# Ternary-weight sums on ScalarE instead of VectorE, and newly drawn instruction orders, in a macaron transformer kernel

## The reference

```
def _quantize(w):
    gamma = jnp.mean(jnp.abs(w))
    return jnp.clip(jnp.round(w / (gamma + EPS)), -1.0, 1.0)
...
x = x + 0.5 * _L0_ffn_ref(_layernorm(x), ...)      # silu(gate) * up, down
x = x + _L0_attn_ref(_layernorm(x), ...)           # 16 heads, rotary, causal
x = x + 0.5 * _L0_ffn_ref(_layernorm(x), ...)
x = x + 0.5 * _L1_ffn_ref(_layernorm(x), w1, w2, w3)   # sigmoid(x1) * x2, ternary
x = x + _L1_attn_ref(_layernorm(x), ...)           # 16 heads on 4 KV heads, alibi
x = x + 0.5 * _L1_ffn_ref(_layernorm(x), w1, w2, w3)
```

## Time and profile before

| | |
|---|---|
| median of 3 runs | 553.93 us (552.02 to 555.36) |
| the profiled execution's own time | 552.14 us |
| its span, first to last instruction | 550.4 us |
| PE busy | 530.6 us (96%) |
| DVE busy | 456.1 us (83%) |
| ACT busy | 401.3 us (73%) |
| POOL busy | 340.8 us (62%) |

### The profile page before, as it was taken

One profiled execution on the slowest core, in us unless ns is written; L12 is line 12 of the kernel. 1 busy time (PEld: TensorE's weight loads), 2 busy tenths in 40 slices (PEclk: granted clock), 3 DMA queues, 4 the chain that ended last, 5 costly groups with the idle time before them and its releaser, 6 DMA issues.

```text
span 550.4 us, 12977 instructions
## 1 busy us (share of the span) xinstructions
PE 530.6 (96%) x5060; PEld 302.9 (55%) x5060; DVE 456.1 (83%) x816; ACT 401.3 (73%) x603; POOL 340.8 (62%) x427
## 2 busy tenths in 40 slices
PE   8999798999999999999899999999999999999997
PEld 6676444445554654566446564465455654654664
DVE  5999999998989797699987969879997779783363
ACT  5978594878777698775886848788769676969443
POOL 2549896975987797673664364552855626545634
PEclk9999999999999999999999999999999999999999
DMA  8900110302130100410110120010211011101211
GB/s 324 355 1 2 58 58 2 116 23 62 41 103 18 43 1 2 157 42 20 63 43 2 42 83 22 22 43 6 75 36 43 1 42 64 52 2 62 80 58 38
DMA packets 22573, 31.76 MB, mean 58 GB/s; under 512 B 9408, under 2 KB 10816, under 8 KB 22360
## 3 DMA queue, kind: packets, MB, share of 16 engines
q1 hardware_dynamic: 22512, 30.94, 16.4%
HBM read 13.75 MB, written 2.36 MB: 29 GB/s over the span
## 4 chain that ended last, share of the span: by engine, by line
PE 71%; DVE 17%; ACT 4%; issue 3%; POOL 2%; SPq 1%; DMA 0%; DVEq 0%; POOLq 0%; ACTq 0%
PE PS L597 22%; PE PS L621 12%; PE PS L708 10%; PE PS L688 5%; PE PS L673 5%; DVE MX L1064 5%; PE PS L639 4%; PE PS L723 4%; PE PS L580 3%; PE PS L544 2%; PE PS L559 2%; ACT PB L850 2%; PE PS L655 2%; DVE MX L1060 1%; DVE ST L875 1%
## 5 line engine op out<-in xcount | busy, mean ns | idle before, releaser
L850 ACT ACTIVATE PB<-PS 128x1024 f32<-128x1024 f32 x160 | 158.7, 1025 | 52.9 <-PE PS L688 48.4
L1064 DVE TENSOR_REDUCE MX<-PS 128x2 f16<-128x1024 f32 (+2 forms) x192 | 158.3, 865 | 13.8 <-PE PS L544 13.1
L597 PE MATMUL PS<-XT,WGU 128*128 128x512 f16 x660 | 156.9, 380 | 4.6 <-DVE QF L1042 3.0
L1140 POOL TENSOR_TENSOR HH<-TH,HH 128x512 f16<-128x512 f32 x71 | 82.5, 1173 | 69.0 <-ACT HH L818 69.0
L1168 POOL TENSOR_SCALAR_AFFINE_SELECT PB<-PB 128x512 f32<-128x512 f32 (+1 forms) x140 | 73.8, 552 | 48.1 <-ACT PB L850 47.9
L597 PEld LDWEIGHTS PS<-XT,WGU 128*128 128x128 f16 x660 | 59.6, 98 | 75.9 <-issue 7.8
L621 PE MATMUL PS<-WD,HH 128*128 128x256 f16 x660 | 78.2, 273 | 0.4 <-POOL HH L1140 0.2
L708 PE MATMUL PS<-PB,V 128*32 128x512 f32 (+3 forms) x1024 | 75.3, 435 | 0.8 <-ACT PB L850 0.3
L621 PEld LDWEIGHTS PS<-WD,HH 128*128 128x128 f16 x660 | 62.6, 98 | 13.3 <-issue 3.3
L818 ACT ACTIVATE HH<-TH 128x512 f16<-128x512 f32 (+1 forms) x86 | 52.9, 628 | 20.2 <-PE PS L621 6.9
L673 PE MATMUL PS<-SK,SQ 63*128 63x256 f16 (+3 forms) x512 | 59.5, 299 | 5.3 <-DVE MX L1064 2.6
(11 more groups left out here) (119 smaller groups left out, 777.7 us busy)
## 6 DMA issues: line engine op xcount, KB each, us to landing
SQ<-QPB SPq DMA_DIRECT2D x24, 256.0 KB, 2.5
OC<-OT SPq DMA_DIRECT2D x16, 256.0 KB, 2.4
RB<-scratch SPq DMA_DIRECT2D x64, 64.0 KB, 2.3
SK<-QPB SPq DMA_DIRECT2D x12, 256.0 KB, 2.4
SQ<-MT SPq DMA_DIRECT2D x128, 1.0 KB
out<-X SPq DMA_DIRECT2D x8, 256.0 KB, 2.1
PB<-gu SPq DMA_DIRECT2D x2, 704.0 KB, 6.1
LATE<-gu SPq DMA_DIRECT2D x2, 704.0 KB, 14.5
```

The lines of the kernel that those rows point to most:

```text
L597: m = e.matmul(o[:, :], WGU[l][:, k, col:col + P], rows_of(f)[j][:, k, :], start=j == 0 and k == 0, stop=j == 1 and k == 1)
L850: e.activation(PB[Q % 2][:, j, :, :], two_banks("s", i), ACT.Exp, scale=0.25).then_inc(a_exp, 1)
L1064: e.tensor_reduce(mx[:, :, pr, t], o[:, :, col:col + (t + 1) * P], AX.X, ALU.max, negate=True).then_inc(a_max, 1)
L1140: e.tensor_tensor(hh[1][:, s * T:(s + 1) * T], value_of(j)[0], hh[0][:, s * T:(s + 1) * T], ALU.subtract).then_inc(f_lo, 1)
```

## The change

The sums of |w| leave VectorE. ScalarE gets a new step `B`, seven times: an activation Abs over a piece of the weights (1024, 256, 256 and four times 704 elements per partition), which writes its values to a place that nobody reads and leaves their sum in one column of `GA` by `accum_out`. A new semaphore `p_abs` counts them, and each waits for the one before. VectorE keeps the short final sums, over 4 and 2 x 2 columns instead of 22 and 2 x 22, so its string has six fewer `w`, and the values of `p_dve` are renumbered. ScalarE's `T`, which loads the table with silu, moves to the front of its string. All strings of `ORDER` and the banks are new: they come out of a search that judges an order under two sets of durations instead of one. The strings differ in places all the way to the end, but hold the same letters otherwise.

```diff
     "pe":
-        "zzzzzzzttzgGgggGGgGtzztgzGzagGgddddggGztzzgzGtGuugGaqqvgddgdvdqgGgqgtGGGguuGtqqqzmmmgmmgqmmdmmGsdsms"
...
+        "zzzzzzzttzzgggGggGzztGtGgGgGazggddddgtgGGtGGzzuuggagqzggqddzgvdGdqqvGGzgGuuGtqqtqmmmmgmqmgmdmmdsGsms"
...
     "act":
-        "wXxxTwttthtXhhthxxhtwwhtthwXthwtxwthYyyxthkhhkkvwQttQXtktvkhtYQyytQhhhxxkkkhhtwTQteQeeeeteewQQhoeete"
...
+        "TwXxxwtttwtXhthhxxBBBththhtXhBwthBwtxtwBBYxyythhhttkhttXQvtQhkkkYtQyyQxvhhhxhkQhktTwwwwQtkeeeeekehtQ"
...
-                w.wait_ge(p_dve, (8, 20)[i])
+                w.wait_ge(p_dve, (5, 13)[i])
...
+                elif c == "B":
+                    if i < 3:
+                        w.wait_ge(l_w3, 32)
+                        src = (rd[0].rearrange("p c n -> p (c n)"), rd[1][:, 0, :], rd[1][:, 1, :])[i]
+                        junk, total = TD[:, 0:(1024, 256, 256)[i]], GA[:, 2, i:i + 1]
+                    else:
+                        k, u = divmod(i - 3, 2)
+                        w.wait_ge(l_w1, 32)
+                        src, junk, total = rgu[k][:, u * HID:(u + 1) * HID], TB[1], GA[:, u, k:k + 1]
+                    w.wait_ge(p_abs, i)
+                    e.activation(junk, src, ACT.Abs, accum_out=total).then_inc(p_abs, 1)
...
-                    elif i <= 2:
-
-                        w.wait_ge(l_w3, 32)
-                        if i == 1:
-                            ga, src = GA[:, 2, 0:16], rd[0]
-                        else:
-                            ga, src = GA[:, 2, 16:20], rd[1][:, 0:1, :]
-                        e.tensor_reduce(ga, src.rearrange("p c (a b) -> p (c a) b", b=64), AX.X, ALU.add,
-                                        apply_absolute_value=True).then_inc(p_dve, 1)
-                    elif i == 3:
-
-                        e.tensor_reduce(GA[:, 2, 20:21], rd[1][:, 1:2, :], AX.XY, ALU.add,
-                                        apply_absolute_value=True).then_inc(p_dve, 1)
-                        w.wait_ge(p_dve, 5)
-                        e.tensor_scalar(GA[:, 2, 21:22], GA[:, 2, 20:21], -0.5, None, ALU.mult).then_inc(p_dve, 1)
-                        w.wait_ge(p_dve, 6)
-                        e.tensor_reduce(GS[:, 2:3], GA[:, 2, :], AX.X, ALU.add).then_inc(p_dve, 1)
-                    elif i in (4, 12):
-
-                        k = 0 if i == 4 else 1
+                    elif i == 1:
+                        w.wait_ge(p_abs, 3)
+                        e.tensor_scalar(GA[:, 2, 3:4], GA[:, 2, 2:3], -0.5, None, ALU.mult).then_inc(p_dve, 1)
+                        w.wait_ge(p_dve, 3)
+                        e.tensor_reduce(GS[:, 2:3], GA[:, 2, 0:4], AX.X, ALU.add).then_inc(p_dve, 1)
+                    elif i in (2, 6):
+
+                        k = 0 if i == 2 else 1
                         c0, c1 = ((2, 3), (0, 2))[k]
                         w.wait_ge(p_pe, k + 1)
                         e.tensor_scalar(GS[:, c0:c1], bank("a", k)[:, c0:c1], 1.0 / (HID * D), 1e-8,
                                         ALU.mult, ALU.add).then_inc(p_dve, 1)
-                        w.wait_ge(p_dve, 8 + 12 * k)
+                        w.wait_ge(p_dve, 5 + 8 * k)
                         e.tensor_scalar(GS[:, 3 + c0:3 + c1], GS[:, c0:c1], -0.5, None, ALU.mult).then_inc(p_dve, 1)
-                        w.wait_ge(p_dve, 9 + 12 * k)
+                        w.wait_ge(p_dve, 6 + 8 * k)
                         e.tensor_scalar(GS[:, c0:c1], GS[:, c0:c1], 0.5, None, ALU.mult).then_inc(p_dve, 1)
-                    elif i <= 6:
-                        k = i - 5
+                    elif i <= 4:
+                        k = i - 3
                         c0, c1 = ((0, 4), (4, 6))[k]
                         src, td = rd[k].rearrange("p c n -> p (c n)"), TD[:, 0:(c1 - c0) * D]
-                        w.wait_ge(p_dve, 10 + 2 * k)
+                        w.wait_ge(p_dve, 7 + 2 * k)
                         e.tensor_scalar(td, src, GS[:, 5:6], None, ALU.is_lt).then_inc(p_dve, 1)
-                        w.wait_ge(p_dve, 11 + 2 * k)
+                        w.wait_ge(p_dve, 8 + 2 * k)
                         e.scalar_tensor_tensor(WD[1][:, c0:c1, :].rearrange("p c n -> p (c n)"), src, GS[:, 2:3],
                                                td, ALU.is_gt, ALU.subtract).then_inc(p_dve, 1)
-                    elif i <= 10:
-                        k, u = divmod(i - 7, 2)
-                        w.wait_ge(l_w1, 32)
-                        e.tensor_reduce(GA[:, u, 11 * k:11 * k + 11],
-                                        rgu[k][:, u * HID:(u + 1) * HID].rearrange("p (a b) -> p a b", b=64),
-                                        AX.X, ALU.add, apply_absolute_value=True).then_inc(p_dve, 1)
-                    elif i == 11:
-                        w.wait_ge(p_dve, 18)
-                        e.tensor_reduce(GS[:, 0:2], GA[:, 0:2, :], AX.X, ALU.add).then_inc(p_dve, 1)
-                    else:
-                        k = i - 13
-                        w.wait_ge(p_dve, 22 + 4 * k)
+                    elif i == 5:
+                        w.wait_ge(p_abs, 7)
+                        e.tensor_reduce(GS[:, 0:2], GA[:, 0:2, 0:2], AX.X, ALU.add).then_inc(p_dve, 1)
+                    else:
+                        k = i - 7
+                        w.wait_ge(p_dve, 15 + 4 * k)
```

More of the change, by code:

```diff
@@ new lines @@
+        "msdsmdmsmgsmmpmssgmsGsmGsspsmGsmgmmpsmsmssgmmsGmmpsmsvmsvsmsmuummpqqoosmsoosssqdmsmdqtsspmmtdgggdGsG"
+        "smmgsmpmsGmsmgssgGGpmsmvmsdsmsdmsmvduudqssmqspmoottomsoggmsgGGgssmGqgmspsmqtmsgtGGpsssggddssddgmmpGG"
+        "gmmmvgvGmmuguGGoooosmqmmsqsmqmsdmsddmdsmsmsmsmspmmsmttsspsmggGgGsmgGggGGsmpmsdttsmddssmdggsmpmsmgGvg"
+        "GuGugsqmmqgGqssooGssmpmmmddddsmsosomsmmpmttsssgGgsgGmsspmsmgsmgGsmmGGgmmspsmsvdmsmddsmsdssmpmsttoosm"
+        "mgoguoguGGsmqsmqgqssmgGgGGsmmpmssdmsdmsmdsmdmpsmssmpsmttvmsggGgGGggGsmgGtsmtddmssddmsmpoosmspsouuogs"
@@ new lines @@
+        "mqmsqgGqgGssspsmmgmsvmGmmpmmggGsmsmsGsmsttmpmssddsmmdgdoooogsmsgGsmgmmmpssGssGggssspsstGGtpggGddddgg"
+        "GGgGgGooooddddttggGggGGgGGgdddd",
+    "dve":
+        "NXgtwtNhhhNktthhwhwhwhdwdknthhNwhtuuhwpqwpqdwdhpnqphqhkhhuuhtpqpqtmmmpmsmhxmmmsmdqmhxmqpmmmdmxmsmkmh"
+        "smhnmxmmsmhmcmxmsmmmhmcmxmmmuumxpqpqomoNpmmdqpqtmtcmxsshshdhmkmmsmhmmxnshshmmmcmxdmmuudNppqmqmottmox"
+        "hmkhhNmpmqhmmxcqphhttssdhdnmmshhcmkmmshmsxmshuhuoommlmmmlxmdlmdmmxNmmmmmttNmhxhkchmhhmhmxttmdmdnssmh"
+        "mmhcksshuushlmmxhsllomhmmdxmdmNommmmttxNhhmhkmmmcxhmhmmhmmxcmmdmdmnmttommxshsoushuhkmmlsllmsxhshhmmm"
+        "mdmmxmdmNmmNmxttcmhhhkhhmchtmtdmxdnmmomuumhlmxohlclkNhmmmmmhxmmmhmmxchmmttmdmmhdkxooNmhmmmmxhhchtthh"
+        "cdhhdkhhhooNdXtthkhhhdhhdd",
@@ new lines @@
+        "6035062403641053753020574757250425261046250362542063510632635730623453062540635603410641367531750432"
+        "1530153730253035152406204625351370514265021563107451250532316434062406304631576240725063214507530626"
+        "0437053204062165426054306715306143610561357015302507405270525032504275310732403516340275306235742507"
+        "4207421357135124062560432064371634760325235012460531706421254063170327341536026043602436053601346024"
+        "60247604025753024062406236406135160315072046024512062413514027561024502530126320360",
@@ L249, in macaron_kernel @@
         l_ali = [sem(f"l_ali{z}") for z in range(2)]
-        p_act, p_pool, p_dve, p_pe, p_set, p_tab, p_sc, p_gu = (sem(f"p_{n}") for n in ("act", "pool", "dve", "pe", "set", "tab", "sc", "gu"))
+        p_act, p_pool, p_dve, p_pe, p_set, p_tab, p_sc, p_gu, p_abs = (sem(f"p_{n}") for n in ("act", "pool", "dve", "pe", "set", "tab", "sc", "gu", "abs"))
         f_ln, f_ve, f_mean, f_rt, f_off, f_xn, f_xd = (sem(f"f_{n}") for n in ("ln", "ve", "mean", "rt", "off", "xn", "xd"))
@@ L564, in tensor_program @@
                     w.wait_ge(p_pool, 3)
-                    w.wait_ge(p_dve, (7, 19)[i])
+                    w.wait_ge(p_dve, (4, 12)[i])
                     c0, c1 = ((2, 3), (0, 2))[i]
@@ L589, in tensor_program @@
                     else:
-                        w.wait_ge(p_dve, 30)
+                        w.wait_ge(p_dve, 23)
                     wait_bank(w, c, i)
```

48 lines of the change are left out of this document (15 added, 33 removed).

## The result

The changed kernel takes 555.51 us (median of 16 executions, 554.46 to 556.42), the kernel before, measured beside it, 553.17 (551.83 to 555.63): ratio 1.0037 [1.0024, 1.0051]. Forecast was 551.0, and a gain. The profiled execution has a span of 553.5 us, 3.1 more than before.

What follows compares the result with a forecast made beforehand. VectorE sets the pace up to 107.8 us, TensorE behind it. Of 5.46 us removed, waits of 0.35, 1.2 and 1.0 leave 2.9: 552.14 becomes 549.2, or 551.0 us on the median's level; range 547.3 to 554.8.

Steps and rivals of the forecast that it cites:

- So of 5.46 us, 5.46 - 0.35 - 1.2 - 1.0 = 2.9 us come through to the first row maximum: VectorE's first stage: 5.46 us of sums removed, less losses at three places, brings the first row maximum 2.9 us sooner.
- POOL and SP have the same steps, and the SP queue the same DMAs ahead of each result; these cost nothing: GpSimd's steps and the DMA queue: unchanged, so no cost if the first attention's row vectors go out as early.
- I take that to stay as it is: Two VectorE threshold scalings at 0.98 us instead of 0.15: assumed unchanged, up to 1.7 us either way.
- the three I walked: Places in the first 45 us where VectorE loses time: 0.35, 1.2 and 1.0 us.
- place 2: VectorE's third gated product waits 1.2 us for TensorE's second G, now its seventh step.
- no row says which, and I take zero: Behind 107.8 us, with new strings: TensorE's 6.8 us idle time may shrink or grow; change taken as zero.
- Place 3: Third unit's transposed rows: VectorE waits about 1.0 us for ScalarE to copy them, at about 37 us.
- The upper bound of 6.6 us: ScalarE's seven sums: most they could add, with a 0.20 us activation for each read-out.
- no row of ScalarE from SBUF is slower than 1.1 ns an element: Argument against slow sums on ScalarE: profile rows show at most 1.1 ns per element from SBUF.
- TensorE's own string is packed up to the first projection: TensorE up to 46.08 us: only 0.30 us of waits, so the projection comes at most 0.3 to 0.4 us sooner.
- The third rival: Slow sums on ScalarE delay the first attention's normalized rows and chain behind; 557.3 us; chance 0.14, shared with later strings.
- The later strings lose: New orders behind 107.8 us add 3.4 us, half the idle 6.8, cancelling the gain; shares the 0.14 chance of slower.

Runs made afterwards that it cites:

- e12: Changed kernel with its first three filler steps written as 4 matmuls of 512 columns instead of 8 of 256, the same work; 553.68 us, ratio 1.0008.
- e18: Changed kernel with 5 instead of 7 fillers ahead of the first transposes; 552.97 us, ratio 1.0001.
- e6: Kernel before with VectorE's sums of |w| reading only a sixteenth of their elements, all else the same; 551.75 us, ratio 0.9979.
- e7: Changed kernel with ScalarE's seven sums cut to 64 elements each, all else the same; 554.94 us, ratio 1.0034.
- e20: Kernel before with only the sums of w1 and w2 moved into ScalarE's gaps and its table load first; 551.71 us, ratio 0.9970.
- e1: Code of the change, all seven sums on ScalarE and table load first, in the strings and banks of the kernel before; 554.40 us, ratio 1.0027.
- e14: Code of the change with the changed kernel's strings up to about 79 us, then those of the kernel before; 557.49 us, ratio 1.0071.
- e15: Code of the change with the strings of the kernel before up to about 79 us, then the changed kernel's; 557.46 us, ratio 1.0075.
- e3: Changed kernel's strings and banks with the sums back on VectorE, ScalarE's table load still first; 561.88 us, ratio 1.0163.

## Why the prediction was wrong

**The step that failed** is "So of 5.46 us, 5.46 - 0.35 - 1.2 - 1.0 = 2.9 us come through to the first row maximum". Measured is 1.58 us more distance. Two things stand in its place, and a third term, taken at zero, adds to them.

*A collision.* "POOL and SP have the same steps, and the SP queue the same DMAs ahead of each result; these cost nothing": the DMAs are the same, but one met a load of instructions, whose place no string shows. That is 1.55 us of distance and 1.6 us of time, by e12; e18 agrees.

*Nothing comes through without it either.* e12's window against that of before above:

```profile
11.05:79.97 68.92, 66.17 (x426) 41.32 (x425) 64.55 (x128) 54.69 (x97) 50.64 (x51) 1.00 0.28 109
```

The distance is the same, 68.92 and 68.89. VectorE is busy for 64.55 instead of 67.51 us: of 5.46 us removed, 2.5 came back in its other steps, and the remaining 2.96 went into idle time, 4.37 instead of 1.38. The first half is the term "I take that to stay as it is", with its bound of 1.7 us: it held two small scalings, and what grew were above all the weight comparisons, by 2.7 us together. The second half is more waits than the three I walked. The 1.49 us for TensorE (place 2) were forecast; 0.4 us each for GpSimd's x, and for ScalarE's rows, and part of a wait for the first transposed rows were not. e6 shows the second half without a new string: with only VectorE relieved, three quarters of the relief turn into its idle time.

*The strings behind.* "no row says which, and I take zero": the profiles have 473.0 us from the first row maximum to the end where before has 471.8, so 1.2 us of the 3.1 us of the longer span lie there. e12, without the collision and with the distance of before, has 553.68 us in 12 executions, all with a mean granted clock of 0.999 or 1.0; the 13 of before beside it at that clock have a median of 552.31. These 1.4 us point the same way. Which steps lose them stays open, and with them T2b.

**The rest, by its steps.** The removed sums and ScalarE's 5.5 us were right, so was the table load; by the ratios of e7 and after (1.0034 and 1.0037), what ScalarE's sums cost the changed kernel can't be told from zero. Place 3, "about 1.0 us" for ScalarE's rows, was wrong: VectorE found them ready. The upper bound of 6.6 us was too high because the read-outs overlap. In "no row of ScalarE from SBUF is slower than 1.1 ns an element" I overlooked the row that the sum itself uses, 0.52 us for 256 elements, 2.0 ns each. "TensorE's own string is packed up to the first projection" was seen but not used: the projection came 36.5 us behind the first transposes, 36.4 before, where I had it 0.3 to 0.4 us sooner.

The third rival, slower by ScalarE's sums, gave the right sign for a wrong reason. "The later strings lose" was right in kind: of its 3.4 us the profiles show 1.2.

## What to carry to other kernels

When one engine is busy for 98% of a stage, look at how full the others are before pricing its relief: here a quarter to a third came through to the first row maximum (e6, e20), and of the two placements of the sums in the old strings the one in ScalarE's gaps gained (e20), the other lost (e1). A change of instruction counts moves the 16 KB loads of instructions; if a transfer on which the next step waits grows a thin tail, look for a load inside it, and shift it by a few instructions. Strings fitted to one set of loads did not survive a splice or a return of the old work here (e14, e15, e3). A difference of 1 us between two profiles can be chance, as e14 shows; go by the medians.
